# A decoder layer on one core: the last chunk's query parts in other buffers, and each shift sent ahead of the next stack in the second attention

## What is computed

```python
x = _layernorm(x + attn(x, qkv_w, proj_w, proj_b, slopes))     # causal-biased self attention
x = _layernorm(x + xattn(x, ctx, ctx, mask, Wq, bq, ...))      # cross attention to 77 context tokens
x = _layernorm(x + ffn(x, rw1, ..., eb2))                      # 8 experts, top 2

# inside xattn
qh = split_heads(q @ Wq.T + bq); kh = split_heads(k @ Wk.T + bk); vh = split_heads(v @ Wv.T + bv)
scores = einsum('bhqd,bhkd->bhqk', qh, kh) / sqrt(16) + mask * -1e15
attn = einsum('bhqk,bhkd->bhqd', softmax(scores), vh)
out = attn.reshape(B, L, 256) @ Wo.T + bo
```

## Time and profile before

| | |
|---|---|
| median of 3 runs (lowest, highest) | 1822.04 us (1821.58, 1823.98) |
| time of the profiled execution | 1818.98 us |
| its span from first to last instruction | 1817.2 us |
| mean granted TensorE clock | 0.933 of full speed |
| TensorE busy (matmul) | 1625.6 us, 89% |
| VectorE, ScalarE, GpSimd busy | 1283.7 us, 1007.0 us, 369.6 us |
| projection stage | 901 to 1009 us of the span |
| second attention, up to its last chunks | 1009 to 1204 us |

### The profile page before, as it was taken

The page is one execution under the profiler, slowest core; times in us unless marked ns, Lnnn a source line. Parts: engine busy times, 40 slices in busy tenths (PEclk is TensorE's granted clock), DMA queues, the critical chain, the costliest instruction groups (busy, mean ns, idle before and its releaser), DMA issues. The chain is left out here.

```text
span 1817.2 us, 36241 instructions
## 1 busy us (share of the span) xinstructions
PE 1625.6 (89%) x14848; PEld 1064.3 (59%) x14848; DVE 1283.7 (71%) x2242; ACT 1007.0 (55%) x1727; POOL 369.6 (20%) x258
## 2 busy tenths in 40 slices
PE   7869999999999999999789688869985999999990
PEld 6734444444444444444378445547764888888890
DVE  6978888888888888888288457652334677877744
ACT  5336777777777777777645267844433233333313
POOL 6540000000000000000012001101552255555521
PEclk9968999999999999999999579969996999999995
DMA  7855444443434444320168866313213244444226
GB/s 244 260 168 96 93 94 90 92 89 86 97 83 69 69 69 70 69 37 8 53 215 212 161 104 124 100 50 113 81 38 113 71 96 97 96 96 97 39 24 196
DMA packets 130516, 184.47 MB, mean 102 GB/s; under 512 B 29466, under 2 KB 93864, under 8 KB 129260
## 3 DMA queue, kind: packets, MB, share of 16 engines
q1 hardware_dynamic: 113584, 153.81, 34.5%
q0 software_dynamic: 13440, 22.07, 5.9%
q10 hardware_dynamic: 3328, 6.29, 2.3%
HBM read 115.43 MB, written 70.06 MB: 102 GB/s over the span
## 5 line engine op out<-in xcount | busy, mean ns | idle before, releaser
L732 DVE TENSOR_REDUCE att_row_max<-att_ring 128x2 f32<-128x1024 f32 x512 | 601.9, 1221 | 108.0 <-PE att_ring L797 76.4
L716 ACT ACTIVATE att_w_exp<-att_s_ps 128x512 f32<-128x512 f32 x1008 | 539.1, 598 | 209.9 <-PE att_s_ps L844 140.4
L871 PE MATMUL att_a_ps<-att_w_exp,att_v_group 128*32 128x512 f32 x2048 | 273.6, 606 | 0.8 <-ACT att_acc_sb L705 0.6
L830 PE MATMUL att_s_ps<-att_q_stack,att_k_stack 62*128 62x512 f32 x640 | 183.6, 478 | 0.0
L830 PEld LDWEIGHTS att_s_ps<-att_q_stack,att_k_stack 62*128 62x128 f32 x640 | 86.1, 184 | 122.2 <-ACT att_w_exp L716 111.9
L2369 ACT ACTIVATE ex_hid<-ex_h_ps,ex_b 128x512 f32<-128x512 f32 x128 | 87.3, 686 | 118.3 <-DVE ex_h_lo L2427 65.4
L2427 DVE TENSOR_TENSOR ex_h_lo<-ex_hid,ex_h_hi 128x512 fp32r<-128x512 f32 x128 | 138.7, 1083 | 4.4
L2320 POOL DMA_INDIRECT x_scr<-ex_y,ex_home x60 | 100.7, 1679 | 176.6 <-DVE ex_y L2417 162.8
L648 POOL COPY att_eyes<-keep_slope_eye 128x384 bf16<-128x384 bf16 x16 | 8.1, 509 | 624.6 <-PE att_s_ps L844 615.6
L844 PE MATMUL att_s_ps<-att_eyes,keep_past_bf 64*128 64x64 bf16 x3786 | 131.7, 193 | 0.0
L797 PE MATMUL att_ring<-att_k_stack,att_q_stack 60*128 60x512 f32 x640 | 125.6, 439 | 5.0 <-DVE att_row_max L732 4.1
(11 more groups left out here) (308 smaller groups left out, 3553.7 us busy)
## 6 DMA issues: line engine op xcount, KB each, us to landing
first_w_raw<-ew SPq DMA_DIRECT2D x16, 1024.0 KB
att_k_stack<-qk_scr SPq DMA_DIRECT2D x40, 256.0 KB
rows_scr<-att_zeros POOLq DMA_DIRECT2D x8, 1040.0 KB, 9.1
first_rows<-rows_scr SPq DMA_DIRECT2D x16, 520.0 KB
qk_scr<-qkv_t_lo SPq DMA_DIRECT2D x14, 512.0 KB, 4.5
qk_scr<-qkv_t_hi SPq DMA_DIRECT2D x14, 512.0 KB, 4.3
keep_k_stack<-qk_scr SPq DMA_DIRECT2D x24, 256.0 KB
att_q_stack<-qk_scr SPq DMA_DIRECT2D x20, 256.0 KB
```

What stands on the lines that cost most here:

```text
L716: nc.scalar.activation(w_exp[(STEPS * g.n + st) % SETS][h][:, :], score_bank(v), ACT.Exp).then_inc(exp_done, 1)
L732: nc.vector.tensor_reduce(out, ring[place.slot][:, :, :], AX.X, ALU.max).then_inc(ring_free, 1)
L830: ins = nc.tensor.matmul(score_bank(v), ks[g.buf][rows, c, j, kt * P:(kt + 1) * P], qs[g.buf][rows, j, c * CH:(c + 1) * CH], start=True, s ...
L871: ins = nc.tensor.matmul(a_ps[32 * h:32 * h + 32, :], vg[g.buf][:, kt, h * VW:h * VW + 32], w_exp[(STEPS * g.n + st) % SETS][h][:, :], sta ...
```

## The change

It does three things.

1. The query parts of chunk 7 get buffers of their own: `parts_of` gives the tiles `att[1]` and `att[2]`, whose attention rows are used up, in place of `q_hi[1]` and `q_lo[1]`. For chunk 7 ScalarE waits for the last transpose of attention rows (`t_done`) and no longer for the stores of chunk 5; VectorE's wait on them goes as well.
2. `att` and `x` are allocated after the keys' tiles, further up, so that the second attention's stacks 2 and 3 no longer lie over `att[1]` and `att[2]`. SyncE waits for all stores of query parts before it loads `x` for chunk 0 of the second attention.
3. In the second attention, SyncE loads the stack of chunk n+3 behind the shift of chunk n+1 and not in front of it, and ScalarE issues its half in step 3 and not in step 0.

```diff
--- before.py
+++ after.py
@@ -1069,8 +1069,6 @@
 
     with Scope(nc, "so") as s:
         ident, w_hi, w_lo, proj_b, bq = (lent[name] for name in ("ident", "w_hi", "w_lo", "proj_b", "bq"))
-        att = [lent["att"]] + [s.sb(f"att{i}", [P, TPC, C], F32) for i in range(1, LOADED)]
-        x = [lent["x"]] + [s.sb(f"x{i}", [P, TPC, C], F32)[:, :, :] for i in range(1, LOADED)]
         a_hi = [s.sb(f"a_hi{i}", [P, CK, CH], F32R) for i in range(2)]
         a_lo = [s.sb(f"a_lo{i}", [P, CK, CH], F32R) for i in range(2)]
         res = [s.sb(f"res{i}", [P, TPC, C], F32) for i in range(2)]
@@ -1097,9 +1095,18 @@
 
         spare = stacks[1][:, :, :].rearrange("p j t -> p (j t)")
         wk_hi, wk_lo = [spare[:, i * 2048:(i + 1) * 2048].rearrange("p (c m) -> p c m", c=CK) for i in range(2)]
+        att = [lent["att"]] + [s.sb(f"att{i}", [P, TPC, C], F32) for i in range(1, LOADED)]
+        x = [lent["x"]] + [s.sb(f"x{i}", [P, TPC, C], F32)[:, :, :] for i in range(1, LOADED)]
 
         q_hi = [s.sb(f"q_hi{i}", [P, CK, CH], F32R) for i in range(2)]
         q_lo = [s.sb(f"q_lo{i}", [P, CK, CH], F32R) for i in range(2)]
+
+        last_hi, last_lo = (att[i][:, :, :].rearrange("p t c -> p (t c)").rearrange("p (k n) -> p k n", k=CK).bitcast(F32R) for i in (1, 2))
+
+        def parts_of(n):
+
+            return (last_hi, last_lo) if n == CHUNKS - 1 else (q_hi[n % 2][:, :, :], q_lo[n % 2][:, :, :])
+
         t_ps = s.pb("t_ps", (P, CK, CH))
         r_ps = s.pb("r_ps", (P, TPC, C))
         t1_ps = s.pb("t1_ps", (P, CK, CH))
@@ -1156,9 +1163,9 @@
 
             def store_q(n):
                 sp.wait_ge(q_lo_done, n + 1)
-                for part, tile in ((0, q_hi[n % 2]), (1, q_lo[n % 2])):
+                for part, tile in enumerate(parts_of(n)):
                     sp.dma_start(io["q2_scr"][n, part * D:(part + 1) * D].rearrange("(k d) h t -> (d h) k t", k=CK),
-                                 tile[:, :, :].bitcast(F32)).then_inc(q_out[n % 2], 16)
+                                 tile.bitcast(F32)).then_inc(q_out[n % 2], 16)
 
             sp.dma_start(att[1][:, :, :], chunk_rows(io["att_scr"], 1)).then_inc(in_done[1], 16)
             load_keys()
@@ -1227,9 +1234,11 @@
 
             def split_q(n):
                 act.wait_ge(q_sum_done, n + 1)
-                if n >= 2:
+                if n == CHUNKS - 1:
+                    act.wait_ge(t_done, CHUNKS)
+                elif n >= 2:
                     act.wait_ge(q_out[n % 2], Q_STORES * (n // 2))
-                nc.scalar.activation(q_hi[n % 2][:, :, :], q_sum[n % 2][:, :, :], ACT.Copy).then_inc(q_hi_done, 1)
+                nc.scalar.activation(parts_of(n)[0], q_sum[n % 2][:, :, :], ACT.Copy).then_inc(q_hi_done, 1)
 
             def split_keys():
                 act.wait_ge(ctx_in, 32)
@@ -1300,9 +1309,11 @@
             def split_q(n):
 
                 dve.wait_ge(q_hi_done, n + 1)
-                dve.wait_ge(q_out[n % 2], Q_STORES * (n // 2))
+                if n < CHUNKS - 1:
+                    dve.wait_ge(q_out[n % 2], Q_STORES * (n // 2))
                 dve.wait_ge(q_lo_done, n)
-                nc.vector.tensor_tensor(q_lo[n % 2][:, :, :], q_sum[n % 2][:, :, :], q_hi[n % 2][:, :, :].bitcast(F32), ALU.subtract).then_inc(q_lo_done, 1)
+                hi, lo = parts_of(n)
+                nc.vector.tensor_tensor(lo, q_sum[n % 2][:, :, :], hi.bitcast(F32), ALU.subtract).then_inc(q_lo_done, 1)
 
             def scale(n):
                 if n >= 2:
@@ -1617,6 +1628,9 @@
             move_top(0)
             sp.wait_ge(ones_in, 96)
             load_ones(sp, io, qst[3], ones_in)
+
+            for c in range(2):
+                sp.wait_ge(q_out[c], Q_STORES * CHUNKS // 2)
             load_x(0)
             sp.dma_start(bo, io["bo"].partition_broadcast(P)).then_inc(weights_in, 16)
             for n in range(CHUNKS + 2):
@@ -1626,12 +1640,12 @@
                         sp.dma_start(lent["router_w"][:, k, :], io["rw1"][k * P:(k + 1) * P, :]).then_inc(lent["router_w_in"], 16)
                     sp.wait_ge(out_done, 16)
                     sp.dma_start(lent["x_send"][:, :, 0:C], chunk_rows(io["x2_scr"][0:T], 0)).then_inc(io["chunk_in"][0], 16)
-                if has(n + 3):
-                    load_stack(n + 3)
                 if 1 <= n < CHUNKS:
                     load_x(n)
                 if has(n + 1):
                     move_top(n + 1)
+                if has(n + 3):
+                    load_stack(n + 3)
                 if has(n - 2):
                     store(n - 2)
             sp.wait_ge(out_done, 16 * CHUNKS)
@@ -1693,10 +1707,10 @@
                         weights(n, u)
                     if u == 0 and has(n - 1):
                         copy_acc(n - 1, 3)
-                    if u == 0 and has(n + 3):
-                        load_stack(n + 3)
                     if u == 2 and has(n + 1):
                         copy_top(n + 1)
+                    if u == 3 and has(n + 3):
+                        load_stack(n + 3)
                     if u == 3 and has(n):
                         copy_acc(n, 0)
                     if u == 4 and has(n - 1):
```

## The result

The changed kernel took 1816.0 us (median of 20 runs, 1803.17 to 1831.28), the kernel before, run beside it, 1822.97 us (20 runs, 1817.0 to 1836.12). The ratio is 0.9956, with 0.9939 to 0.9974 as its 95% interval: 8.0 us faster by the ratio (4.7 to 11.1), 7.0 by the medians. Forecast was 6.1. The profiled execution took 1812.77 us against 1818.98, its span was 1811.0 against 1817.2, the mean granted clock 0.936 against 0.933.

What follows compares the result with a forecast made beforehand. No engine was full; waits at single points between barriered stages bound the two stages. -4.4 + 1.4 - 3.4 + 0.3 = -6.1 us, giving 1815.9 us against the median of 1822.04, range 1811.5 to 1820.5.

Steps and rivals of the forecast that it cites:

- ScalarE's wait: Projection's end: chunk 7's rounding no longer waits for chunk 5's stores, so the second attention starts 4.4 us earlier.
- Given back before the first scores: Between barrier and first scores: DMA traffic limits the first shift, so 1.4 us of the earlier start is lost.
- about 6: Expected sign: the first scores start 3 us earlier, so the wait before them is about 6 us, not 4.6.
- Chunk 1's wait: Second attention: with SyncE's stack load behind the second shift, chunk 1's scores no longer wait for it, 3.4 us gained.
- the new situation: Second shift's write: only ScalarE's half of a stack in flight, so it lands in 3.3 us like the third.
- ScalarE's issue: Step 3, chunks 2 to 4: some 0.1 us of issuing shows before the copy of `acc`, 0.3 us lost.
- the second in about as long: ScalarE's stack issue in step 3: the first DMA takes 0.55 us beside the exponentials, the second about as long.
- Stacks in time: Later chunks of the second attention: stacks sent later still arrive before they are wanted, stack 4 by 2.4 us; nothing charged.
- with the 8.2 us that such a load took: SyncE's half of stack 4, started at 1065.2, takes 8.2 us and is there at 1073.4.
- The second rival: Stacks come late in chunks 4 to 7; at 13.5 us per load 8.9 us is lost, total 1824.8; chance 0.12.
- The clock at the start: Barrier before the second attention: the clock falls to 1.2 GHz as before, so nothing is charged or credited.
- The rival of the swallowed start: DMA queue swallows the earlier start: first scores still start at 1031, total 1818.9 us; chance 0.16.

Runs made afterwards that it cites:

- `x1` later: The changed kernel with the wait for the last `x1` store moved from the projection's end to the second attention, ahead of the first shift: 1822.47 us, one run.
- the first shift by ScalarE: The changed kernel with the first shift's write issued by ScalarE and not by SyncE behind stack 2: 1820.36 us, ratio 0.998 to the kernel before.
- its sister with `x1` later: The changed kernel with ScalarE's stack halves in step 0 and the wait for `x1`'s stores behind the barrier: 1817.4 us, ratio 0.9966 to the kernel before.

## Why the prediction was right

The total was right: 6.1 forecast, 8.0 measured (4.7 to 11.1). Step by step:

- **ScalarE's wait, -4.4.** Right. It is gone whole, and where the barrier is free the maxima start 4.35 to 4.40 earlier (buffers alone; `x1` later). In the change itself they start 3.8 earlier: SyncE's wait for chunk 7's `x1`, whose store was issued at 992.15 and took 13.4 us, was next in line and held the barrier 0.6; in six of nine traces it held nothing. The forecast hadn't asked what else SyncE waits for there.
- **Given back before the first scores, +1.4 with ends 0 and 4.4.** As a size, right within its ends; as a number, not a constant. In the change it was 0 behind the barrier, so the scores came 3.8 earlier and not 3.0, and the wait before the scores 4.68 where "about 6" was written; in the buffers-only kernel 1.7, with a wait of 6.36, and there in the reading back and not in the write, to which the forecast had put it. Over all kernels with the new buffers the first scores started 24.4 to 28.6 us from the anchor.
- **Chunk 1's wait, -3.4.** Right: gone in every kernel with SyncE's half behind the shift (-3.7 in the table). The write took 1.6 us, half of the 3.3 taken from the third shift, because ScalarE's half went out behind it: what the forecast took for the new situation, that half in flight, was not the change's. Where it was in flight the write took 3.6 to 7.1, and was in time too.
- **ScalarE's issue, +0.3.** Mis-sized. The step "the second in about as long" took 0.55 us for both issues; the second took 0.63 to 1.21. In chunk 3 the idle is 0.15, as estimated, but in chunk 2 0.73, with 0.4 to 0.6 on the path (the projection at 9.0 and not 8.6 or, at the high clock, 8.4). The loss of 4.9 us in chunk 2, which may come from this through the clock, was in no term.
- **Stacks in time, 0.** Failed, in small. The step "with the 8.2 us that such a load took" was wrong: of two halves that overlap, SyncE's took 11.2 and 13.7, and stack 4 was 1.55 late. The second rival put its threshold at 10.6 and gave 2.9 for 13.5; 1.55 was paid at stack 4 and nothing at the others. Their margin may be owed to chunk 2's loss, which came before them: in the kernel where that loss is absent and ScalarE's other halves are late, one later stack was 0.64 late; but with the first shift by ScalarE one was 1.06 late behind the same loss.
- **The clock at the start.** Right in the outcome: it fell, and 42 us of matmuls in the next 50 didn't raise it. The reason given, a fall at 1002 inside an idle stretch that ends at 1004.9, was not what happened: it fell after 1005, later than that end, and still ahead of the first maxima at 1006.12. That was luck. But it came back at 1056, 50 us after the first maxima, and before 54 after them; in other kernels up to 79 later (1083). A forecast from one trace can't price that.

That the net comes out is in part luck. In the trace the two gains were 7.5 where 6.4 was forecast; then stack 4 cost 1.0 and chunk 2 4.9, the stage's end gave 3.4 and the stages behind it 1.4, none of it forecast. One reading of the earlier trace rows was wrong without effect on the sum: in the projection VectorE is busy 81.6 us, more than TensorE's 80.9 and not less. The split was less right. By whole runs the buffers alone bring 0.9962 (3.0 us faster forecast, 2.7 to 11.3 faster measured) and the order alone 0.9999 (3.1 faster forecast, between 4.6 faster and 4.2 slower measured). So what can be shown in the median comes from the buffers; the order's gain is plain in the traces, up to the third shift, and not in the runs. The rival of the swallowed start is refuted by the buffers-only kernel (2.6 of 4.4 arrive) and that of late stacks by its size.

The best ratio was that of SyncE's half late with ScalarE's in step 0 (0.9937 [0.9915, 0.9959]). It is the version I would keep, since it has the shift's gain, no late stack and no issue in front of the copy of `acc`; but its interval overlaps the change's, and its sister with `x1` later gave 0.9966, so that it beats the change isn't shown.

## What to carry to other kernels

When a wait in front of a barrier goes, list every engine's last waits there: the next one was 0.6 us behind in one execution and not on the path in most. Take a load's duration from a row in which the same transfers overlap as they will afterwards; 8.2 us became 13.7 when both halves of a stack went out together. And an issue on an engine that others follow step by step is not free because its engine is busy anyway: leave it where the engine waits for someone else.

## What the runs showed of the hardware

- TensorE's clock stayed at 1.2 GHz for 50 to 54 us with 42 us of matmuls in them, in the change and before, and up to 1083 in one execution. Where the clock fell 6.9 to 7.9 us after the fourth shift's copy, four traces with a delay of 0.5 to 0.6 us on ScalarE had a low stretch of 17 us, and four without it one of 3.4, with TensorE busy in all of either. I expected such a delay to cost what it lasts. How long the clock is low after the barrier differs widely between traces of kernels that are alike up to there, so a few us of difference between two traces need not be the change's.
- The issue of a DMA on ScalarE's queue took 0.55 to 1.33 us. The second of a stack's two took 0.96 to 1.33 in step 3 of chunk 2, in all five kernels that have it there, and 0.63 for stack 3.
- A store of 64 KB landed in 1.6 us with nothing in front of it, in up to 7.9 with some loads in flight, from either queue (the first shift's: 4.2 to 6.9 from SyncE's, 5.6 to 7.0 from ScalarE's), in 10.2 behind SyncE's half of a stack and in 13.3 to 14.1 behind both halves.
